# A rotation in two pieces: the scalar engine exchanges the halves, one product with a full sine table replaces two

## The chip, the cores and the metric

The kernel runs on one core of one Trainium2 chip. The metric is the device time of one execution in microseconds; times below are the median of three runs, and the time and span of one profiled execution. Engines: TensorE (PE, with its weight loads as PEld), VectorE (DVE), ScalarE (ACT), GpSimd (POOL), SyncE (SP, which here only issues transfers).

## What is computed

Four layers, each `x = x + attention(ln(x)) * silu(ffn(ln(x)))`, on 2 sequences of 512 tokens with 256 features. The change lies in the third layer's attention (and its entry), which has 16 query heads of width 128 in 4 groups; a group shares one key and one value head:

```python
q = einsum("bim,ghmd->bghid", x, w_aq); k = einsum("bim,gmd->bgid", x, w_ak); v = ...
def _rope(x):                      # angles: position * 10000 ** (-arange(64) / 64)
    even, odd = split(x, 2, axis=-1)           # two halves of 64 features
    return concatenate([even * cos - odd * sin, even * sin + odd * cos], axis=-1)
s = einsum(_rope(q) * c, _rope(k) * c) - 1e30 * (later key)      # c = 128 ** -0.25
p = softmax(s); o = einsum(p, v); r = einsum(o, w_ao)
```

## The kernel before, in words

Each engine runs a list of instructions written out by hand; semaphores order them across engines, and an instruction that waits holds back all that stands behind it on its engine.

**Steps and units.** The third attention (`attention2` on each engine) works in 32 units, one for each head and sequence, of four steps; a step u handles 128 queries against (u % 4 + 1) * 128 keys. A step passes through: scores on PE (L1126), the row maximum on DVE (`maximum`, L2259, whose result `nm` is read out by a second instruction), exp on ACT (`exponent`, L1715), the reciprocal and scaling on DVE (`inverse`, L2274 and L2276), the turn of the probabilities on PE (`turn`, L1130) and a copy on ACT (`store_pt`, the copy helper L1567). After the fourth step PE multiplies with the values (`values`, L1135), and ACT copies the result (`store_output`, L1567) at the start of the next unit. Scores run four steps ahead of turns, so a unit's four score tiles belong to the next unit.

**Projections.** q, k and v of later units are projected inside the steps, at the list positions in `EVENT2`: a q at the fourth step of a unit for three units later (until unit 28), and at the second step of four of the eight units of a group a k or a v of the next group (groups 0 to 2). All of them go through PSUM bank 7, so a projection waits (`free`) until the one before it has been read. Units are called here plain (only a q), k units (k and q: 2 in a group) and v units (v and q: 2 in a group).

**The rotation** of a projected q or k (`rotate2`, L2286 to L2290) is four instructions on DVE, placed at the end of its step: a 128x512 product with the cosines out of PSUM, two 64x512 products with the sines that read the other half of the rows out of PSUM, and the 128x512 sum in SBUF. PE waits for the third (`rope_mul`) before it uses bank 7 again.

The order of the queues in a step u is: PE `turn(u)`, `scores(u + 4)`, a projection if there is one, `values(u)` in a fourth step; ACT `exponent(u + 3)`, `store_output` in a first step, `store_v` for a v projected in the step before, `store_pt(u)`; DVE `inverse(u + 2)`, `maximum(u + 4)`, `rotate2` if there is a projection.

**The entry.** The second layer ends with eight output tiles in `shared1`: PE (L1534) makes a tile, DVE adds (`tail`, L2495), ACT takes the silu (L1897), DVE updates X (`update`, L2478 and L2479). After four tiles DVE takes the statistics of the first half (`ln_stats`, L1971 and L1974), POOL the root (`ln_rstd`, L583 and L584), DVE scales the first half (`ln_scale`, L1981). PE turns this half (`ln_transpose`, L808) ahead of the last two output tiles, and ACT copies it (`ln_copy`) between two silus. Then the second half goes the same way, while PE projects the first sequence's q, k, v (L1119, L1112) and DVE rotates. POOL splits the turned tokens into high and low parts (L734, L735; the sum of both is used from the second head on), and later every q and k weight (L739, L740).

Of the kernel before, what the change touches and what calls it, by code (L numbers as in the profile page):

```python
# [22 lines left out]
ALU = mybir.AluOpType  # L23
# [16 lines left out]
DH = 128  # L40
# [23 lines left out]
def build(nc, W, out):  # L64
    ctx = ExitStack()
    with ctx:
# [16 lines left out]
        def sem(name):  # L83
            return ctx.enter_context(nc.semaphore(name))
# [54 lines left out]
        spare2 = W2[:, 7168:10240]  # L139
        ks2 = [ks, [spare2[:, 512 * b:512 * b + 512] for b in range(B)]]  # L140
        vv2 = [vv, [spare2[:, 1024 + 512 * b:1536 + 512 * b].rearrange("p (j e) -> p j e", j=TPB) for b in range(B)]]
        rope_t = [ropet, spare2[:, 2048:2560]]
        rope_u = [ropeu, spare2[:, 2560:3072]]

# [166 lines left out]
        corea = [{k: sem(f"{k}_{l + 2}") for k in CORE_A + (() if l == 0 else ("pj_used", "w_parts"))} for l in range(2)]  # L311
        wq_in, wk_in, wv_in = sem("wq_in"), sem("wk_in"), sem("wv_in")
        xl_ready, parts_2 = sem("xl_ready"), sem("parts_2")
        rope_mul, qk_ready, v_ready = sem("rope_mul"), sem("qk_ready"), sem("v_ready")
        ot_ps, ot_sb, out_ps, s_ready = sem("ot_ps"), sem("ot_sb"), sem("out_ps"), sem("s_ready")
        comb_out, comb_in = sem("comb_out"), [sem(f"comb_in_{i}") for i in range(2)]
# [100 lines left out]
        def nth_qk(e):  # L417

            return sum(1 for x in PJ2[:e] if x[0] != "v")
# [147 lines left out]
        def _(pool):  # L567
            steps = [0]

            def own(ins):  # L570

                steps[0] += 1
                ins.then_inc(pool_step, 1)
                pool.wait_ge(pool_step, steps[0])
# [156 lines left out]
            for b in range(B):  # L731
                t = slice(b * SEQ, (b + 1) * SEQ)
                pool.wait_ge(xnt_ready, LN_PAIRS * 2 + 2 * (b + 1))
                own(pool.tensor_copy(XH2[:, :, t], XNT[:, :, t]))  # L734
                pool.tensor_tensor(XL2[:, :, t], XNT[:, :, t], plain(XH2[:, :, t]), ALU.subtract).then_inc(parts_2, 1)  # L735
            for kind, i in SPLIT2:
# [59 lines left out]
        def _(pe):  # L796
# [373 lines left out]
            def attention2():  # L1170
                ca = corea[0]

                def free(e):

                    kind = PJ2[e][0]
                    if kind == "v":
                        pe.wait_ge(v_ready, nth_v(e) + 1)
                    else:
                        pe.wait_ge(rope_mul, nth_qk(e) + 1)

                def project(e):
                    kind, b, i, bank = PJ2[e]
# [329 lines left out]
            def shared1():  # L1512
                f = ffn[1]
                nm = len(SH1)
                for b in range(B):
                    for n, (c0, r) in enumerate(SH1):
                        k = b * nm + n
                        i = k % 2
                        if k >= 2:
                            pe.wait_ge(f["h"], k - 1)  # L1520
                        for s in range(2):
                            for c in range(DC):
                                ins = mm(PS[2 * s + i][0:r, :], sgu1[:, s, c, c0:c0 + r], XNT[:, c, b * SEQ:(b + 1) * SEQ],  # L1523
                                         start=c == 0, stop=c == DC - 1)
                        ins.then_inc(f["gu_ps"], 1)
                pe.wait_ge(s_ready, NT * 2)
                pe.wait_ge(f["h"], B * nm)
                for m in range(NT):
                    if m == NT - 2:
                        ln_transpose(2, (0, 1))  # L1530
                    if m >= 2:
                        pe.wait_ge(f["f"], m - 1)
                    for n, (c0, r) in enumerate(SH1):
                        ins = mm(PS[6 + m % 2][:, 0:D], h1[0:r, n, m * P:(m + 1) * P], sd1[0:r, n, :],  # L1534
                                 start=n == 0, stop=n == nm - 1)
                    ins.then_inc(f["y_ps"], 1)

            for l in range(4):
                if l == 0:
# [23 lines left out]
        def _(act):  # L1563
# [8 lines left out]
            def ln_copy(l, pairs=range(LN_PAIRS)):  # L1572

                for k in pairs:
                    act.wait_ge(xnt_ps, LN_PAIRS * l + k + 1)
                    src = PS[turn_bank(l, k)][:, :].rearrange("p (m c t) -> p c m t", m=2, c=DC)
                    dst = (XH3 if l == 3 else XNT)[:, :, 2 * k * P:(2 * k + 2) * P].rearrange("p c (m t) -> p c m t", m=2)
                    copy(dst, src).then_inc(xnt_ready, 1)
# [143 lines left out]
            def attention2():  # L1722
                ca = corea[0]

                def exponent(u):
                    act.wait_ge(ca["nm"], u + 1)
                    if u >= 4:
                        act.wait_ge(ca["pt_ps"], u - 3)
                    exp_tile(u).then_inc(ca["e_ready"], 1)

                def store_pt(u):
                    unit = u // TPB
                    act.wait_ge(ca["pt_ps"], u + 1)
                    if u % TPB == 0 and unit >= 2:
                        act.wait_ge(ca["o_ps"], unit - 1)
                    copy_pt(u, unit % 2).then_inc(ca["pt_sb"], 1)

                def store_v(e):
                    kind, b, i, bank = PJ2[e]
                    if kind == "v":  # L1740
                        act.wait_ge(ca["pj_ps"], e + 1)
                        copy(vv2[i % 2][b].rearrange("p j e -> p (j e)"), PS[bank][:, :]).then_inc(v_ready, 1)

                def store_output(unit):
                    head, b = unit // B, unit % B
                    act.wait_ge(ca["o_ps"], unit + 1)
                    copy(OT23[:, head, b * SEQ:(b + 1) * SEQ], PS[6][:, :]).then_inc(ca["o_used"], 1)

                store_v(2)
                ln_copy(2, (2, 3))  # L1750
                for u in range(3):
                    exponent(u)
                store_v(5)
                for u in range(STEPS2):
                    if u + 3 < STEPS2:
                        exponent(u + 3)
                    if u % TPB == 0 and u > 0:
                        store_output(u // TPB - 1)
                    if u - 1 in EVENT2:
                        store_v(EVENT2[u - 1])  # L1760
                    store_pt(u)
                store_output(NH * B - 1)

# [195 lines left out]
        def _(dve):  # L1959
# [303 lines left out]
            def attention2():  # L2263
                ca = corea[0]
                dve.wait_ge(ld["ffn2"], 32)

                def maximum(u):
                    dve.wait_ge(ca["s_ps"], u + 1)
                    max_tile(u).then_inc(ca["nm"], 1)

                def inverse(u):
                    c = u % 4
                    dve.wait_ge(ca["e_ready"], u + 1)
                    own(dve.reciprocal(erec[:, c:c + 1], esum[:, c:c + 1]))  # L2274
                    p = Pr[c][:, 0:(u % TPB + 1) * P]
                    ts(p, p, erec[:, c:c + 1], None, ALU.mult).then_inc(ca["p_ready"], 1)  # L2276

                def rotate2(e):

                    kind, b, i, bank = PJ2[e]  # L2280
                    if kind == "v":
                        return
                    n, x, hf = nth_qk(e), PS[bank], DH // 2
                    t, u = rope_t[n % 2], rope_u[n % 2]
                    dve.wait_ge(ca["pj_ps"], e + 1)
                    tt(t, x[:, :], rope2[:, 0, :], ALU.mult)  # L2286
                    tt(u[0:hf, :], x[hf:, :], rope2[hf:, 1, :], ALU.mult)
                    tt(u[hf:, :], x[0:hf, :], rope2[0:hf, 1, :], ALU.mult).then_inc(rope_mul, 1)
                    dve.wait_ge(rope_mul, n + 1)
                    tt(qs[b] if kind == "q" else ks2[i % 2][b], t, u, ALU.add).then_inc(qk_ready, 1)  # L2290

                rotate2(0)
                ln_scale(2, 1)
                rotate2(1)
                rotate2(3)
                rotate2(4)
                for u in range(4):
                    maximum(u)
                inverse(0)
                inverse(1)  # L2300
                for u in range(STEPS2):
                    if u + 2 < STEPS2:
                        inverse(u + 2)
                    if u + 4 < STEPS2:
                        maximum(u + 4)
                    if u in EVENT2:
                        rotate2(EVENT2[u])

# [358 lines left out]
def shape_tables():  # L2667
# [20 lines left out]
    c = DH ** -0.25  # L2688

    t["rope2"] = np.ascontiguousarray(np.stack([np.concatenate([np.cos(ang), np.cos(ang)], 0) * c,  # L2690
                                                np.concatenate([np.sin(ang), -np.sin(ang)], 0) * c], 1)).astype(np.float32)
    t["desc"] = np.tile((E - np.arange(E)).astype(np.float32), (P, 1))
    return t

# [54 lines left out]
```

## Time and profile before

| | us |
|---|---|
| median of 3 runs (lowest to highest) | 1256.98 (1256.3 to 1258.65) |
| profiled execution, its own time | 1254.57 |
| its span (and what lies around it) | 1252.8 (1.8) |
| PE, DVE, ACT busy in the span | 1154.7 (92%), 730.0 (58%), 592.1 (47%) |
| entry and third attention: from the last tiles of the second layer to the last unit's values | about 453 to 749 |

The share of busy time is an average over four layers. What the change is worth is read from the entry and from the 32 units: where one engine waits for another there, and for how long.

### The profile page before, as it was taken

The numbers are of one execution on the slowest core, as the hardware profiler recorded it, in microseconds if no ns is written. First come the engines' busy times: TensorE is split into PE (matmuls) and PEld (weight loads), VectorE is DVE, ScalarE is ACT, GpSimd is POOL, SyncE is SP. The second block draws the span as 40 slices with busy tenths as digits, with TensorE's granted clock in tenths as the row PEclk, the third lists the DMA queues.
The fourth block names the chain that finished last, engine by engine and source line by source line (L and its number), as shares of the span: only waits on it lengthen the run. The fifth ranks groups of instructions, "written<-read, shape, count | busy, mean of one in ns | idle before, by whom it ended". The sixth has DMA issues, their size and how long they took to land.

```text
span 1252.8 us, 18479 instructions
## 1 busy us (share of the span) xinstructions
PE 1154.7 (92%) x6272; PEld 788.1 (63%) x6276; DVE 730.0 (58%) x2031; ACT 592.1 (47%) x1494; POOL 211.1 (17%) x265
## 2 busy tenths in 40 slices
PE   5979988988999978999999999999999999999999
PEld 4635454523267555666767668877777777776877
DVE  2878726846234278989898853434444444446574
ACT  1735553677832223455545543415555555555140
POOL 3150013521500413000100012010211021110000
PEclk9989999999999998999999999999999999999999
DMA  8001100050222500000000010220000000000001
GB/s 231 35 2 48 49 30 1 11 177 1 70 82 81 185 0 18 13 14 9 13 9 10 9 68 26 78 86 9 22 22 17 18 26 18 19 9 2 0 1 34
DMA packets 26896, 48.66 MB, mean 39 GB/s; under 512 B 3774, under 2 KB 20126, under 8 KB 25734
## 3 DMA queue, kind: packets, MB, share of 16 engines
q1 hardware_dynamic: 24070, 38.13, 9.5%
q0 software_dynamic: 2736, 9.37, 2.6%
q8 instruction: 52, 0.85, 0.3%
q14 instruction: 38, 0.31, 0.1%
HBM read 40.36 MB, written 9.19 MB: 40 GB/s over the span
## 4 chain that ended last, share of the span: by engine, by line
PE 73%; DVE 15%; ACT 6%; issue 4%; POOL 1%; DMA 1%; SPq 0%; ACTq 0%; DVEq 0%; POOLq 0%
PE bank L1135 9%; PE bank L1126 8%; PE bank L1319 8%; PE bank L1130 5%; PE bank L1364 4%; PE bank L1233 4%; PE bank L1314 4%; PE bank L1194 3%; PE bank L1472 2%; PE bank L1039 2%; PE bank L1028 2%; ACT PT L1686 2%; PE bank L1523 2%; PE bank L1490 2%; PE bank L949 1%
## 5 line engine op out<-in xcount | busy, mean ns | idle before, releaser
L2259 DVE CUSTOM_DVE_ANT_0 bank<-bank,mask_row 128x128 f32<-128x128 f32 (+3 forms) x256 | 126.7, 496 | 147.5 <-PE bank L1126 147.0
L1567 ACT COPY R<-bank 128x512 f32<-128x512 f32 (+5 forms) x175 | 94.9, 555 | 217.5 <-PE bank L1135 123.5
L1715 ACT ACTIVATE R<-bank,nm 128x128 f32<-128x128 f32 (+3 forms) x256 | 136.3, 532 | 112.7 <-DVE nm L2259 111.6
L1126 PE MATMUL bank<-R 128*128 128x512 f32 (+3 forms) x384 | 134.3, 434 | 0.0
L1567 ACT COPY PT<-bank 128x128 f32<-128x128 f32 (+3 forms) x256 | 108.5, 425 | 22.9 <-PE bank L1130 22.9
L1130 PE MATMUL bank<-identf,R 128*128 128x128 f32 x640 | 112.2, 274 | 6.2 <-DVE R L2276 6.1
L1130 PEld LDWEIGHTS bank<-identf,R 128*128 128x128 f32 x640 | 79.2, 141 | 37.5 <-DVE R L2276 20.0
L1135 PE MATMUL bank<-PT,R 128*128 128x512 f32 (+3 forms) x256 | 74.7, 435 | 5.9 <-ACT PT L1567 5.9
L1686 ACT ACTIVATE PT<-bank 128x512 f32<-128x512 f32 x128 | 66.5, 608 | 14.1 <-PE bank L1028 14.1
L1135 PEld LDWEIGHTS bank<-PT,R 128*128 128x128 f32 x256 | 47.5, 189 | 35.1 <-issue 15.4
L2161 DVE TENSOR_REDUCE W<-bank 128x1 f32<-128x128 f32 (+3 forms) x128 | 57.0, 485 | 17.7 <-PE bank L905 16.8
L2276 DVE TENSOR_SCALAR R<-R,erec 128x128 f32<-128x128 f32 (+3 forms) x128 | 56.1, 438 | 5.2
L1126 PEld LDWEIGHTS bank<-R 128*128 128x128 f32 x384 | 58.2, 191 | 1.4 <-issue 0.8
L1675 ACT ACTIVATE PT<-bank 128x512 f32<-128x512 f32 (+3 forms) x128 | 45.8, 437 | 25.4 <-PE bank L938 25.2
L1233 PE MATMUL bank<-W,R 128*128 128x256 f32 x256 | 55.8, 379 | 0.4 <-ACT R L1567 0.4
L1364 PE MATMUL bank<-W,R 128*128 128x256 f32 x256 | 55.8, 379 | 0.4 <-ACT R L1567 0.4
L2322 DVE TENSOR_SCALAR R<-R,erec 128x128 f32<-128x128 f32 (+3 forms) x128 | 52.7, 412 | 5.1
L1364 PEld LDWEIGHTS bank<-W,R 128*128 128x128 f32 x256 | 48.4, 190 | 7.1 <-issue 0.6
L1233 PEld LDWEIGHTS bank<-W,R 128*128 128x128 f32 x256 | 48.4, 190 | 7.1 <-issue 0.6
L1028 PE MATMUL bank<-R 96*128 96x512 bf16 x128 | 42.1, 392 | 11.0 <-ACT PT L1686 7.2
L1715 ACT ACTIVATION_READ_ACCUMULATOR R<-bank,nm 128x1 f32 x256 | 50.4, 197 | 0.0
L1028 PEld LDWEIGHTS bank<-R 96*128 96x128 bf16 x128 | 10.5, 97 | 55.7 <-ACT PT L1686 50.1
(363 smaller groups left out, 2524.0 us busy)
## 6 DMA issues: line engine op xcount, KB each, us to landing
W<-in_wq SPq DMA_DIRECT2D x32, 128.0 KB, 2.0
W<-in_wo SPq DMA_DIRECT2D x2, 2048.0 KB, 8.1
W<-in_egu SPq DMA_DIRECT2D x1, 2816.0 KB
W<-in_wk SPq DMA_DIRECT2D x20, 128.0 KB, 2.0
R<-xg SPq DMA_DIRECT2D x5, 512.0 KB, 4.6
yg<-R SPq DMA_DIRECT2D x5, 512.0 KB, 3.3
W<-in_wa SPq DMA_DIRECT2D x2, 1024.0 KB, 5.4
W<-in_wb SPq DMA_DIRECT2D x2, 1024.0 KB, 7.1
```

Of the source, the lines that this page charges most:

```text
L1028: mm(PS[n % 3][:, :], kstk[0:KQ, g, b * SEQ + j * P:b * SEQ + (j + 1) * P], qstk[0:KQ, g * GH + h, b * SEQ:(b + 1) * SEQ], start=True, sto ...
L1126: return mm(PS[u % 4][:, 0:n], q[:, t * P:n], k[:, 0:n], start=True, stop=True)
L1130: ins = tr(PS[4 + u % 2][:, j * P:(j + 1) * P], Pr[u % 4][:, j * P:(j + 1) * P], identf[:, :])
L1135: ins = mm(PS[6][:, j * P:SEQ], v[:, j, :], PT[:, slot, j, j * P:SEQ], start=j == 0, stop=j == TPB - 1)
L1233: ins = mm(PS[OUT_BANK2[m]][:, 0:D], OT23[:, k, m * P:(m + 1) * P], wo23[:, k, :], start=k == 0, stop=k == NH - 1)
L1319: ins = mm(bank[:, :], w[:, c, :], x[:, c, b * SEQ:(b + 1) * SEQ], start=c == 0 and k == 0, stop=c == DC - 1 and k == 2)
L1364: ins = mm(PS[OUT_BANK3[m]][:, 0:D], OT23[:, k, m * P:(m + 1) * P], wo23[:, k, :], start=k == 0, stop=k == NH - 1)
L1567: return nc.scalar.copy(dst, src)
L1686: fn(PT[:, s % 2, h, :], PS[n % 3][:, :], ACT.Exp, scale=HD ** -0.5).then_inc(cb["pb_ready"], 1)
L1715: return fn(Pr[c][:, 0:n], PS[c][:, 0:n], ACT.Exp, scale=-1.0, bias=nm[:, c:c + 1], accum_out=esum[:, c:c + 1])
L2161: dve.tensor_reduce(nmx[b][:, t, h:h + 1], PS[banks[i % len(banks)]][:, 0:(t + 1) * P], AX.X, ALU.max, negate=True).then_inc(smax_used, 1)
L2259: return dve.tensor_tensor_reduce(out=s[:, 0:n], in0=s[:, 0:n], in1=mask_row[:, SEQ - n:SEQ], scale=-1.0, scalar=-MASKED, op0=ALU.add, op1 ...
```

## The change

The rotation is cut in two. `rotate2` keeps only the product with the cosines. ACT copies the two halves of the projected tile, exchanged, out of bank 7 into a buffer (`swap_halves`, two 64x512 copies, after the cosine product and after the step's `store_pt`). `rotate2_rest`, two steps later on DVE, multiplies that buffer by a full 128-row sine table (one 128x512 product, all in SBUF) and adds. The next projection into the bank now also waits for the two copies (`swap_ready`). At the entry the first transposes stand behind the last two output tiles, POOL's first split waits until all tokens are scaled, and the first four rotations are reordered with the copies among ACT's.

```diff
@@ POOL: split of the tokens
                 pool.wait_ge(xnt_ready, LN_PAIRS * 2 + 2 * (b + 1))
+                pool.wait_ge(xn_ready, NT * 3)
                 own(pool.tensor_copy(XH2[:, :, t], XNT[:, :, t]))
@@ PE: free(e), before a bank is used again
                         pe.wait_ge(rope_mul, nth_qk(e) + 1)
+                        pe.wait_ge(swap_ready, 2 * nth_qk(e) + 2)
@@ PE: shared1
                 for m in range(NT):
-                    if m == NT - 2:
-                        ln_transpose(2, (0, 1))
...
                     ins.then_inc(f["y_ps"], 1)
+                ln_transpose(2, (0, 1))
@@ ACT: attention2
+                def swap_halves(e):
+                    kind, b, i, bank = PJ2[e]
+                    if kind != "v":
+                        n, hf = nth_qk(e), DH // 2
+                        act.wait_ge(rope_mul, n + 1)
+                        if n >= 2:
+                            act.wait_ge(qk_ready, n - 1)
+                        copy(swapped[n % 2][0:hf, :], PS[bank][hf:, :]).then_inc(swap_ready, 1)
+                        copy(swapped[n % 2][hf:, :], PS[bank][0:hf, :]).then_inc(swap_ready, 1)
+
+                swap_halves(0)
+                swap_halves(1)
                 store_v(2)
                 ln_copy(2, (2, 3))
+                swap_halves(3)
+                swap_halves(4)
...
                     if u - 1 in EVENT2:
                         store_v(EVENT2[u - 1])
+                        if PJ2[EVENT2[u - 1]][0] != "v":
+                            store_pt(u)
+                            swap_halves(EVENT2[u - 1])
+                            continue
                     store_pt(u)
@@ DVE: attention2
-                    t, u = rope_t[n % 2], rope_u[n % 2]
-                    dve.wait_ge(ca["pj_ps"], e + 1)
-                    tt(t, x[:, :], rope2[:, 0, :], ALU.mult)
-                    tt(u[0:hf, :], x[hf:, :], rope2[hf:, 1, :], ALU.mult)
-                    tt(u[hf:, :], x[0:hf, :], rope2[0:hf, 1, :], ALU.mult).then_inc(rope_mul, 1)
+                    t = rope_t[n % 2]
+                    if n >= 2:
+                        dve.wait_ge(qk_ready, n - 1)
+                    dve.wait_ge(ca["pj_ps"], e + 1)
+                    tt(t, x[:, :], rope2[:, 0, :], ALU.mult).then_inc(rope_mul, 1)
+
+                def rotate2_rest(e):
...
+                    t, u = rope_t[n % 2], rope_u[n % 2]
+                    dve.wait_ge(swap_ready, 2 * n + 2)
+                    own(tt(u, swapped[n % 2], rope2[:, 1, :], ALU.mult))
                     dve.wait_ge(rope_mul, n + 1)
                     tt(qs[b] if kind == "q" else ks2[i % 2][b], t, u, ALU.add).then_inc(qk_ready, 1)

                 rotate2(0)
                 ln_scale(2, 1)
                 rotate2(1)
+                rotate2_rest(0)
+                rotate2_rest(1)
                 rotate2(3)
                 rotate2(4)
+                rotate2_rest(3)
+                rotate2_rest(4)
...
                         maximum(u + 4)
+                    if u - 2 in EVENT2:
+                        rotate2_rest(EVENT2[u - 2])
                     if u in EVENT2:
                         rotate2(EVENT2[u])
```

The sine table's two halves change sign to match, and the exchange buffer `swapped` (two of 128x512) takes free room in W2. The `own` helper makes DVE wait for its own instruction's end.

## Rows read from the trace of the kernel before

**Rows 1.** Stretch of units: start:end, length, busy PE, PEld, DVE, ACT, POOL; PEclk, DMA.

```profile
500.00:570.00 70.00, 66.39 (x315) 45.87 (x314) 61.39 (x178) 35.94 (x108) 6.55 (x10) 1.00 0.04 12
```

**Rows 2.** Timeline of PE: where `values` starts (start, us, idle before in brackets).

```profile
494.98 2.42 PE L1135 MATMUL bank<-PT,R 128*128 128x512 f32 x8 [1.18 <-ACT PT L1567]
...
537.33 2.32 PE L1135 MATMUL bank<-PT,R 128*128 128x512 f32 x8
545.92 2.32 PE L1135 MATMUL bank<-PT,R 128*128 128x512 f32 x8
...
561.39 2.32 PE L1135 MATMUL bank<-PT,W 128*128 128x512 f32 x8
571.11 2.42 PE L1135 MATMUL bank<-PT,W 128*128 128x512 f32 x8 [1.19 <-ACT PT L1567]
...
693.71 2.32 PE L1135 MATMUL bank<-PT,W 128*128 128x512 f32 x8
...
731.10 2.42 PE L1135 MATMUL bank<-PT,W 128*128 128x512 f32 x8 [0.67 <-ACT PT L1567]
```

**Rows 3.** Timeline of all engines in one plain unit.

```profile
703.82 0.69 DVE L2290 TENSOR_TENSOR R<-R 128x512 f32<-128x512 f32 x1
703.85 0.59 ACT L1567 COPY R<-bank 128x512 f32<-128x512 f32 x1 [1.97 <-PE bank L1135]
...
704.33 0.27 ACT L1567 COPY PT<-bank 128x128 f32<-128x128 f32 x1
...
705.09 0.55 PE L1130 MATMUL bank<-identf,R 128*128 128x128 f32 x3 [0.30 <-DVE R L2276]
...
706.11 0.16 DVE L2274 RECIPROCAL erec<-esum 128x1 f32<-128x1 f32 x1
...
706.51 0.56 DVE L2259 CUSTOM_DVE_ANT_0 bank<-bank,mask_row 128x384 f32<-128x384 f32 x1
...
707.16 0.58 ACT L1715 ACTIVATE R<-bank,nm 128x384 f32<-128x384 f32 x1
...
707.74 0.58 ACT L1567 COPY PT<-bank 128x512 f32<-128x512 f32 x1
```

**Rows 4.** Groups by form, 484 to 737 us (count, busy us, mean ns, idle before).

```profile
L1567 ACT COPY R<-bank 128x512 f32<-128x512 f32 x33 | 19.3, 585 | 57.2 <-PE bank L1135 57.2
...
L740 POOL TENSOR_TENSOR wq_low<-W,wq_high 128x256 fp32r<-128x256 f32 x14 | 13.3, 953 | 1.1
...
L2287 DVE TENSOR_TENSOR W<-bank,W 64x512 f32<-64x512 f32 x18 | 12.5, 692 | 0.2
```

**Rows 5.** Timelines of DVE, ACT and PE at the entry.

```profile
457.07 1.38 DVE L1981 TENSOR_SCALAR XN<-X,mv,rstd 128x256 f32<-128x256 f32 x4 [0.55 <-POOL rstd L584]
461.86 0.48 DVE L2495 SCALAR_TENSOR_TENSOR R<-bank,sgate,PT 128x256 f32<-128x256 f32 x1 [3.41 <-PE bank L1534]
...
466.70 0.38 DVE L1974 BATCH_NORM_AGGREGATE mv<-stat 128x2 f32<-128x6 f32 x4
...
469.99 3.39 DVE L1981 TENSOR_SCALAR XN<-X,mv,rstd 128x256 f32<-128x256 f32 x4
...
460.35 0.42 ACT L1897 ACTIVATE R<-R 128x256 f32<-128x256 f32 x1
...
475.43 6.74 PE L1119 MATMUL bank<-XNT,W 128*128 128x512 f32 x8 [0.68 <-ACT XNT L1567]
```

**Rows 6.** Timeline of POOL at the entry.

```profile
467.48 1.04 POOL L584 TENSOR_TENSOR rstd<-rstd,mhalf 128x4 f32<-128x4 f32 x1
...
469.60 2.66 POOL L735 TENSOR_TENSOR x_low<-XNT,x_high 128x1024 fp32r<-128x1024 f32 x1
```

**Rows 7.** TensorE's clock: a PE timeline row, two windows (PEclk third from the end).

```profile
64.86 3.40 PE L840 MATMUL bank<-identb,PT 128*96 128x128 bf16 x32 [2.55 <-DVE PT L2089]
...
66.00:68.00 2.00, 2.00 (x22) 2.00 (x20) 0.56 (x1) 1.66 (x2) 2.00 (x1) 0.50 0.00 0
...
476.00:478.00 2.00, 2.00 (x3) 0.67 (x2) 0.11 (x1) 0.00 (x0) 1.92 (x2) 0.50 0.03 8
```

More of the change, by code:

```diff
@@ L141, in build @@
         vv2 = [vv, [spare2[:, 1024 + 512 * b:1536 + 512 * b].rearrange("p (j e) -> p j e", j=TPB) for b in range(B)]]
+        swapped = [W2[:, 6144 + 512 * i:6656 + 512 * i] for i in range(2)]
         rope_t = [ropet, spare2[:, 2048:2560]]
@@ L313, in build @@
         xl_ready, parts_2 = sem("xl_ready"), sem("parts_2")
+        swap_ready = sem("swap_ready")
         rope_mul, qk_ready, v_ready = sem("rope_mul"), sem("qk_ready"), sem("v_ready")
@@ L2282, in rotate2 @@
                         return
-                    n, x, hf = nth_qk(e), PS[bank], DH // 2
+                    n, x = nth_qk(e), PS[bank]
+                    t = rope_t[n % 2]
[4 more added lines that the diff above has]
+                def rotate2_rest(e):
+                    kind, b, i, bank = PJ2[e]
+                    if kind == "v":
+                        return
+                    n = nth_qk(e)
                     t, u = rope_t[n % 2], rope_u[n % 2]
-                    dve.wait_ge(ca["pj_ps"], e + 1)
-                    tt(t, x[:, :], rope2[:, 0, :], ALU.mult)
-                    tt(u[0:hf, :], x[hf:, :], rope2[hf:, 1, :], ALU.mult)
-                    tt(u[hf:, :], x[0:hf, :], rope2[0:hf, 1, :], ALU.mult).then_inc(rope_mul, 1)
+                    dve.wait_ge(swap_ready, 2 * n + 2)
+                    own(tt(u, swapped[n % 2], rope2[:, 1, :], ALU.mult))
                     dve.wait_ge(rope_mul, n + 1)
@@ L2690, in shape_tables @@
     t["rope2"] = np.ascontiguousarray(np.stack([np.concatenate([np.cos(ang), np.cos(ang)], 0) * c,
-                                                np.concatenate([np.sin(ang), -np.sin(ang)], 0) * c], 1)).astype(np.float32)
+                                                np.concatenate([-np.sin(ang), np.sin(ang)], 0) * c], 1)).astype(np.float32)
     t["desc"] = np.tile((E - np.arange(E)).astype(np.float32), (P, 1))
```

## The prediction

> **What bounds the kernel now.** I read the busy time by stretches first. In the units PE is busy 66.4 of 70 us, DVE 61.4, ACT 35.9 [rows 1]: PE is the bound, DVE is close behind it, ACT has room, and there are only some 3.6 us of idle PE in 70 to be won. Then the timeline of PE at the value products, which end a unit: from 494.98 to 693.71 lie 24 units (three groups of eight, 66.24 each), from there to 731.10 five more (37.39) [rows 2]. A k unit takes 9.72, of which PE idles 1.19 waiting for the copy of the turned probabilities [rows 2] (the row at 571.11); a v unit takes 8.59 with no idle time (537.33 to 545.92) [rows 2]. With two of each in a group, 29.6 are left for the four plain units, 7.4 each. The third view is all engines in one plain unit [rows 3], where I follow the order of the queues; the fourth, the entry on DVE, ACT and PE [rows 5], where DVE idles 3.41 for output tiles that stand behind the transposes.
>
> **The entry.** With the transposes moved back, the last two tiles are ready before DVE asks for them, so the 3.41 of idle time go [rows 5]. Next comes the silu of the sixth tile, which ACT takes only after copying the transposes, at 460.35 [rows 5]. Before, the addition at 461.86 was followed after 4.84 by the aggregate of the statistics (466.70). If the chain now starts from the silu's end (460.77) without the addition's own 0.40, the aggregate comes at 465.2, 1.5 earlier; without the gap PE should turn and ACT copy 0.75 sooner. I take 2.2 between (bounds 1.5 and 2.3). POOL's root ended at 468.52, but the scaling began only at 469.99 because four rotation instructions stood ahead [rows 5, 6]; one is left, 1.4 gained. The scaling took 3.39 beside POOL's split (469.60, 2.66 long), 1.38 where POOL rested [rows 5, 6]: with the split held back, 2.0. Holding it back delays the split little (it starts with the scaling's end, about 467.8 against 468.5), and its user, the second head's projection, is over 10 us away. Against this, from the scaling's end to the second sequence's projections at 475.43 passed 2.05; now one product (0.65), two copies (1.10), the copy of v (0.48) and the two transposed copies (1.07) follow in turn, 3.3, so 1.25 is given back. After the projections (6.75) DVE needed 2.8 for the last rotation; now one product and two rests follow, about 3.5: another 0.7 back. Sum 2.2 + 1.4 + 2.0 - 1.25 - 0.7 = 3.7 gained (bounds 2.9 and, with the clock below, 6.7).
>
> In the first unit the rotation no longer stands before the maxima; the idle 1.18 at 494.98 [rows 2] goes, as the copies end before PE wants the bank: 1.3 with the shorter first product, bounds 0 and 1.5.
>
> **The rotation in the units.** Removed: two 64x512 products of 0.69 (L2287) [rows 4]; added on DVE: one product from SBUF, 0.69 by the nearest row, the sum of the same form (L2290) [rows 3]. DVE's gain of 0.7 per rotation is worth only what PE's idle time is. Added on ACT: two copies of 64x512. No row has one; a 128x512 copy takes 0.585 [rows 4], and the next starts 0.48 after it (703.85 to 704.33) [rows 3]. From below, half the rows might cost half (0.29); but 64-row products cost DVE the same 0.69 as the 128-row sum [rows 3, 4]. I take the full price: 0.48 + 0.585 = 1.07 for the pair. The Trainium skill (ScalarE: Activation LUTs, What ACT_TABLE_LOAD costs) prices an instruction by the elements in a row alone, 186 ns and 0.833 ns for each, less 93 ns between neighbours: 1.13 for the pair as an estimate, which would add 1.7 to the sum below.
>
> Where the copies stand decides. A q is projected just before the values; its copies stand on ACT behind the output copy and the first probabilities' copy of the next unit. Both wait for PE: the output copy starts at 703.85, when the values have ended. So the pair can't start before about 704.53 (704.33 and 0.20 for the small copy) and ends at 705.60.
>
> What waits for it first is PE. In a k or v unit the k or v projection is next in the bank. PE is through with its first turns and scores by 704.79 (the turn at 705.09 less its idle 0.30 [rows 3]), somewhat sooner in a stream, so it stands for 0.9 to 1.0. Before, the third product had ended by the values' end. A v unit becomes 8.59 + 1.0 = 9.6. A k unit loses its old wait and gets this: 9.72 - 1.19 + 0.95 = 9.5.
>
> What waits second is DVE. In a plain unit the rest stands behind the second maximum and ahead of the third; behind it are an inverse and that maximum, behind the maximum the third exp, behind this on ACT the copy of the fourth probabilities, and for that copy the values wait. That closes a ring from one output copy to the next:
>
> 0.48 output copy + 0.20 small copy + 1.07 exchange + 0.04 + 1.34 rest (two of 0.69, neighbours overlapping) + 0.40 inverse (706.11 to 706.51) + 0.65 maximum to exp (706.51 to 707.16) + 0.58 exp (to 707.74) + 0.58 copy + 0.05 + 2.42 values after a wait + 0.04 = 7.85 [rows 2, 3].
>
> The unit shown takes about 7.4, and PE's own work in it is under 7. After a unit whose values didn't wait it is 0.1 less; mean in a group 7.75. Before, the same ring had no exchange in it: the rotation ran under the values, and nothing after them waited for ACT.
>
> So a group is 2 x 9.5 + 2 x 9.6 + 4 x 7.75 = 69.2, 3.0 more than 66.24; three groups 8.9. The five units after them, each with an exchange left over, take 39.3 against 37.4, 1.9. The last unit has none. Together 10.8 lost, less 3.7 and 1.3: 5.8. Profiled time 1254.57 + 5.8 = 1260.4. The median of the runs shown is 2.4 above the profiled time, so the forecast is 1256.98 + 5.8 = **1262.8**. A link that is 0.1 longer or shorter moves 17 plain units, 1.7; with the entry's bounds this gives 1259.5 to 1267 for this case.
>
> The new sine product reads both operands from SBUF, the two old ones read one from PSUM. For the first two rests POOL's split runs beside them; even at the scaling's ratio (3.39 to 1.38) they are done before the last projections end, which hides it.
>
> **Rivals.**
> - *Half the rows cost half* (faster). If the exchange takes 0.53 instead of 1.07, PE's stand shrinks by 0.54 in 12 units (6.5), and the rest starts 0.28 earlier in 17 (then the second maximum binds it, 4.8): 5.8 - 11.3 = -5.5, 1251.5. It decides from a pair of about 0.87 on, 0.2 less than I take. Against it, the 64-row products. Chance 0.17.
> - *TensorE stays at 2.4 GHz in the entry.* At 476 to 478 the granted clock was 0.50, that is 1.2 GHz, after PE stood idle [rows 7]; now it stands idle for about 2.0, works 1.2 and idles 2.7 ahead of those projections. If the clock holds, they take some 3 less: +2.8, 1259.8. But it also fell, to 0.50 at 66 to 68, around a gap of 2.55 (the row at 64.86) [rows 7]. Chance 0.15. In the units the gaps stay near 1, and with 1.19 the clock was 1.00 [rows 1, 2].
> - *POOL blocks the rest.* 14 splits of 0.95 [rows 4]; if each met a rest and took 0.75 per us, as the split did from the scaling, +10: 1273. Against it, they should run in the unit's first microseconds, before the rest. The Trainium skill (SBUF — State Buffer, Who interferes with whom) has a DVE instruction with two SBUF operands blocked while GpSimd reads SBUF; 3.39 against 1.38 shows such a loss, for another form. Chance 0.08.
>
> **How the numbers follow.** The ring has 0.55; 0.05 is for what I don't see. The range, 1253 to 1269, leaves out most of the first rival and the third, about 2 in 10. A measurement here tells 0.2%, 2.5 us, from no change. Faster 0.18 (the first rival), same 0.19 (half of the second, the ring's lower end), slower 0.63.
>
> **What would show it.** Right: the exchange's copies at 0.58 each, right behind the first small copy; PE waiting for ACT's copies 12 times for about 1.0 before k and v projections; value products waiting about 0.9 for ACT in plain units, spaced 7.75 to 7.85; DVE's idle time ahead of the rest; the scaling at 1.4. Wrong: copies of 0.3, value products 7.0 to 7.4 apart, or the second projections in the entry at full clock.

## The result, and the profile after

The changed kernel takes 1268.85 us (median of 8 runs, 1265.36 to 1274.68), the kernel before 1256.64 beside it (8 runs, 1255.51 to 1259.06): a ratio of 1.0102, 95% interval [1.0083, 1.0121]. That is 12.2 us slower between the medians, where 5.8 were forecast. The direction was right; the forecast size was a little under half of the measured one. The median lies inside the stated range, 1253 to 1269, just under its upper end.

The profiled execution took 1271.36 (its span is 1269.5), 16.8 more than the one before. I cut both traces at the same places: the first aggregate of the statistics at the entry, the first value product, the value products that end the 24 units and the next five, and the end of the span.

| us | before | after | difference | forecast |
|---|---|---|---|---|
| start to the first aggregate | 454.99 | 454.65 | -0.3 | 0 |
| from there to the first values (entry, first unit) | 39.99 | 37.01 | -3.0 | -5.0 |
| 24 units | 198.73 | 214.69 | +16.0 | +8.9 |
| five more units | 37.39 | 40.19 | +2.8 | +1.9 |
| the rest of the kernel | 521.65 | 523.00 | +1.3 | 0 |

The differences add up to the 16.8. This execution lies 2.5 above the median of its own runs, and the one before lay 2.1 below, so 16.8 and 12.2 don't contradict each other. The start, up to the first aggregate, where no edit lies, takes from 450.25 to 455.00 in the eleven traces of this document. So comparisons below go by stretches inside a trace.

The timeline of PE after, at value products and at one v projection:

```profile
491.66 2.32 PE L1138 MATMUL bank<-PT,R 128*128 128x512 f32 x8
...
608.60 2.32 PE L1138 MATMUL bank<-PT,W 128*128 128x512 f32 x8
613.01 2.02 PE L1115 MATMUL bank<-W,XNT 128*128 128x128 f32 x16 [1.11 <-issue]
618.53 2.32 PE L1138 MATMUL bank<-PT,W 128*128 128x512 f32 x8
...
706.35 2.42 PE L1138 MATMUL bank<-PT,W 128*128 128x512 f32 x8
714.38 2.42 PE L1138 MATMUL bank<-PT,W 128*128 128x512 f32 x8
...
746.54 2.42 PE L1138 MATMUL bank<-PT,W 128*128 128x512 f32 x8 [1.24 <-ACT PT L1570]
```

These answer to [rows 2]. A v unit (608.60 to 618.53) takes 9.93 where it took 8.59, and PE, which had no idle time in it, waits 1.11 in front of the v projection. A plain unit (706.35 to 714.38) takes 8.03.

Busy time in the same stretch of units as [rows 1], and in four microseconds of the first unit (PEclk third from the end):

```profile
500.00:570.00 70.00, 62.23 (x294) 42.53 (x295) 49.52 (x152) 44.87 (x124) 5.74 (x10) 1.00 0.04 12
484.00:488.00 4.00, 4.00 (x14) 3.13 (x14) 1.62 (x7) 1.77 (x8) 0.00 (x0) 0.57 0.02 4
```

PE's busy time falls from 66.4 to 62.2 of 70 and DVE's from 61.4 to 49.5, while ACT's grows from 35.9 to 44.9. The work went from DVE to ACT as meant, all three engines now have room, and the units are longer: they wait for one another. The second row shows a fall of TensorE's granted clock (0.57) in the first unit, where the trace of before has 1.00; it lies in the entry's row of the table. Another (0.59 from 860 to 864), which the trace of before doesn't have either, lies in the last row.

All engines in one plain unit after, which answers to [rows 3]:

```profile
716.84 0.58 ACT L1570 COPY R<-bank 128x512 f32<-128x512 f32 x1 [1.80 <-PE bank L1138]
717.33 0.27 ACT L1570 COPY PT<-bank 128x128 f32<-128x128 f32 x1
717.62 1.19 ACT L1570 COPY W<-bank 64x512 f32<-64x512 f32 x2
718.83 0.37 ACT L1718 ACTIVATE R<-bank,nm 128x128 f32<-128x128 f32 x1
718.84 0.69 DVE L2318 TENSOR_TENSOR R<-W 128x512 f32<-128x512 f32 x1 [0.36 <-ACT W L1570]
719.19 0.36 ACT L1570 COPY PT<-bank 128x256 f32<-128x256 f32 x1
719.70 0.63 PE L1133 MATMUL bank<-identf,R 128*128 128x128 f32 x4 [0.79 <-ACT PT L1570]
720.57 0.56 DVE L2280 CUSTOM_DVE_ANT_0 bank<-bank,mask_row 128x384 f32<-128x384 f32 x1
721.22 0.58 ACT L1718 ACTIVATE R<-bank,nm 128x384 f32<-128x384 f32 x1 [0.83 <-DVE nm L2280]
721.79 0.58 ACT L1570 COPY PT<-bank 128x512 f32<-128x512 f32 x1
722.42 0.30 PEld L1138 LDWEIGHTS bank<-PT,W 128*128 128x128 f32 x2 [0.29 <-ACT PT L1570]
722.42 2.42 PE L1138 MATMUL bank<-PT,W 128*128 128x512 f32 x8
```

The ring of the prediction can be followed here: output copy 716.84, small copy 717.33, exchange 717.62, rest 718.84, third maximum 720.57, exp 721.22, copy 721.79, values 722.42, and the next output copy at 724.88, 8.04 later. Two links are longer than forecast: the exchange starts 0.29 behind the small copy and not 0.20, and the rest 1.22 behind the exchange's start and not 1.11. The others agree within 0.05.

But the values wait only 0.29 here (the row of their weight loads), where 0.9 was forecast. PE spends the rest of the waiting earlier, 0.79 ahead of the fourth step's turns (719.70), for a copy of probabilities that stands behind the exchange on ACT. The waits that ended last, for 500 to 753 (us, times, longest):

```profile
PE bank L1133 <- ACT PT L1570: 13.4, 17, 0.8
...
PE bank L1115 <- issue: 6.7, 6, 1.1
...
PE bank L1198 <- issue: 5.6, 5, 1.1
```

The lower two are PE's stand for the bank, ahead of v (L1115) and k projections (L1198); the profile names nothing there, but with one copy less a v unit is 0.61 shorter (experiment 7). The first, 17 times 0.8, was not in the forecast. The chain that ended last, for 716 to 723, goes through it and not through DVE at all:

```profile
717.33 0.27 ACT PT L1570
...
718.23 0.58 ACT W L1570
...
719.29 0.27 ACT PT L1570
...
719.70 0.63 PE bank L1133 x4
720.33 0.86 PE bank L1129 x2
721.18 1.37 PE bank L1198 x6
722.56 0.56 PE bank L1138
```

So there is a second ring: output copy, small copy, exchange, the first exp and the second tile's copy of the next step on ACT, then PE's turns, scores, projection and values, and the output copy again. Both rings pass through the exchange. Which of them holds the unit is what the experiments had to tell.

### The profile page after: what moved, and what is told of

It reads as the page before. It is cut to its first block, busy times and chain, and to the rows that moved or that the text cites. A ratio compares the mean times of both kernels' runs of the same rounds, so it can differ in the third digit from the quotient of the medians.

```text
span 1269.5 us, 18637 instructions
## 1 busy us (share of the span) xinstructions
PE 1159.2 (91%) x6272; PEld 786.4 (62%) x6276; DVE 705.2 (56%) x1991; ACT 635.3 (50%) x1574; POOL 207.7 (16%) x265
## 4 chain that ended last, share of the span: by engine, by line
PE 76%; DVE 8%; ACT 7%; issue 6%; POOL 1%; DMA 1%; SPq 0%; ACTq 0%; DVEq 0%; POOLq 0%
PE bank L1138 11%; PE bank L1129 8%; PE bank L1323 8%; PE bank L1368 4%; PE bank L1237 4%; PE bank L1133 4%; PE bank L1198 4%; PE bank L1318 4%; PE bank L1476 2%; PE bank L1042 2%; PE bank L1031 2%; ACT PT L1689 2%; PE bank L1527 2%; PE bank L1494 2%; PE bank L952 1%
## 5 line engine op out<-in xcount | busy, mean ns | idle before, releaser
L1133 PEld LDWEIGHTS bank<-identf,R 128*128 128x128 f32 x640 | 78.9, 141 | 49.5 <-issue 35.1
L1689 ACT ACTIVATE PT<-bank 128x512 f32<-128x512 f32 x128 | 66.4, 610 | 14.1 <-PE bank L1031 14.1
L1570 ACT COPY W<-bank 64x512 f32<-64x512 f32 (+2 forms) x92 | 53.3, 580 | 38.5 <-PE bank L914 22.9
L2182 DVE TENSOR_REDUCE W<-bank 128x1 f32<-128x128 f32 (+3 forms) x128 | 57.0, 486 | 17.8 <-PE bank L908 17.0
L2297 DVE TENSOR_SCALAR R<-R,erec 128x128 f32<-128x128 f32 (+3 forms) x128 | 53.1, 415 | 5.0
L2358 DVE TENSOR_SCALAR R<-R,erec 128x128 f32<-128x128 f32 (+3 forms) x128 | 52.7, 412 | 5.1
```

Source lines behind the costliest of these rows:

```text
L1133: ins = tr(PS[4 + u % 2][:, j * P:(j + 1) * P], Pr[u % 4][:, j * P:(j + 1) * P], identf[:, :])
L1570: return nc.scalar.copy(dst, src)
L1689: fn(PT[:, s % 2, h, :], PS[n % 3][:, :], ACT.Exp, scale=HD ** -0.5).then_inc(cb["pb_ready"], 1)
L2182: dve.tensor_reduce(nmx[b][:, t, h:h + 1], PS[banks[i % len(banks)]][:, 0:(t + 1) * P], AX.X, ALU.max, negate=True).then_inc(smax_used, 1)
```

## The experiments

The theories, as numbered in the expectations: **A**, one ring, through the rest on DVE (the prediction's); **B**, a second ring of nearly the same length through ACT and PE alone; **C**, it is PE's wait for the bank that matters, and the plain units follow from it. Lengths are means of the distances between value products in the profiled execution (6 k, 12 plain, 6 v units, then five); "entry" is from the first aggregate to the first values. The medians are from several sets of runs: the kernel before took 1256.66 beside experiments 1 to 4, 1254.35 beside 5, 6, 7 and 9, and 1255.2 (one run) beside 8.

| kernel | entry | k | plain | v | last five | time, median |
|---|---|---|---|---|---|---|
| before | 39.99 | 9.90 | 7.32 | 8.58 | 7.48 | 1256.64 |
| changed | 37.01 | 9.73 | 8.03 | 9.99 | 8.04 | 1268.85 |
| entry edits only | 34.90 | 9.98 | 7.32 | 8.58 | 7.47 | 1249.2 |
| rotation only | 39.64 | 9.74 | 8.03 | 9.98 | 8.04 | 1274.44 |
| copies first | 37.23 | 8.79 | 7.58 | 8.63 | 7.53 | 1247.74 |
| rest late | 36.93 | 9.64 | 7.91 | 9.93 | 7.75 | 1266.08 |
| both moves | 36.85 | 8.32 | 7.50 | 8.59 | 7.04 | 1242.45 |
| both, old entry rotations | 33.48 | 8.33 | 7.49 | 8.59 | 7.05 | 1239.25 |
| one copy | 35.11 | 9.02 | 7.56 | 9.38 | 7.61 | 1249.19 (one run) |
| same rows | 37.03 | 9.57 | 7.91 | 9.85 | 7.91 | 1268.08 (one run) |
| split late | 40.24 | 9.73 | 8.00 | 9.99 | 8.04 | 1270.11 (one run) |

**1. The entry edits alone**, in the kernel before: the transposes behind the last output tiles, and POOL's wait.

```diff
@@ POOL
+                pool.wait_ge(xn_ready, NT * 3)
@@ shared1
-                    if m == NT - 2:
-                        ln_transpose(2, (0, 1))
...
+                ln_transpose(2, (0, 1))
```

> The kernel before with two of the entry edits alone: the first transposes behind the last output tiles, POOL's split after the scaling; the rotation stays as before, four instructions on DVE. If these two edits make the entry shorter by themselves: the first unit's values some 4 us earlier than before, units as before, about 1252.5 us. If the gain at the entry needs the shorter first rotation too (the scaling then still stands behind four products): 1 us earlier at most, 1255 to 1257.

Measured 1249.2 (1246.04 to 1253.0), ratio 0.9951 [0.9932, 0.9971]; the entry is 5.1 shorter (some 4 were expected), the units are as before. The two entry edits are a gain by themselves, and with the exchange the entry is 2.1 longer than with them alone. The trace doesn't show where the other 2.4 of the 7.5 between the medians lie.

**2. The rotation alone**, without those two edits.

```diff
@@ POOL
-                pool.wait_ge(xn_ready, NT * 3)
@@ shared1
+                    if m == NT - 2:
+                        ln_transpose(2, (0, 1))
...
-                ln_transpose(2, (0, 1))
```

> The changed kernel without those two edits. If the loss lies in the units and the two edits gain 2 to 4 us: units 18 to 19 us longer than before, slower than the changed kernel by 2 to 4, 1271 to 1274 us. If part of the loss came from the entry's order: 1266 or less.

Measured 1274.44 (1270.14 to 1275.67), ratio 1.0138 [1.0111, 1.0165]; the units as in the changed kernel, to 0.01. It is 5.6 slower than the changed kernel, where 2 to 4 were expected. The loss is the rotation's, and the parts add: 17.8 lost here less 7.5 won in experiment 1 (by the medians of those runs) is 10.3, beside 12.2.

**3. The copies first**: ACT makes the exchange ahead of the output copy and the small copy, under the values.

```diff
@@ ACT: attention2
+                    if u - 1 in EVENT2:
+                        swap_halves(EVENT2[u - 1])
                     if u % TPB == 0 and u > 0:
                         store_output(u // TPB - 1)
                     if u - 1 in EVENT2:
                         store_v(EVENT2[u - 1])
-                        if PJ2[EVENT2[u - 1]][0] != "v":
-                            store_pt(u)
-                            swap_halves(EVENT2[u - 1])
-                            continue
                     store_pt(u)
```

> The changed kernel with ACT's two copies ahead of the output copy and of the turned probabilities' copy, right after the exp, so that they run under the values. Theory A (one ring: exchange, rest on DVE, maximum, exp, copy, values): plain units 7.5, v units 8.6, k units 8.5 to 8.8, about 1245 us. Theory B (a second ring of the same length on ACT alone: exchange, exp of the first tile, copy of the second, turn of the fourth): the same here, as both lose the exchange. Theory C (only the bank wait costs): plain units stay at 8.0, v units 8.6, 1256.

Measured 1247.74 (1245.84 to 1249.75), ratio 0.9927 [0.9903, 0.9951]. The timeline of ACT and PE there:

```profile
694.40 2.42 PE L1138 MATMUL bank<-PT,W 128*128 128x512 f32 x8 [0.32 <-ACT PT L1570]
695.08 1.18 ACT L1570 COPY W<-bank 64x512 f32<-64x512 f32 x2
696.86 0.58 ACT L1570 COPY R<-bank 128x512 f32<-128x512 f32 x1 [0.59 <-PE bank L1138]
...
701.93 2.42 PE L1138 MATMUL bank<-PT,W 128*128 128x512 f32 x8 [0.32 <-ACT PT L1570]
```

The same two copies cost the same 1.18, but they lie under the values, and ACT still rests 0.59 before the output copy. A v unit falls to 8.63 and most plain ones to 7.53, not to 7.0 or so: the ring through the rest still stands, without the exchange (experiment 5 opens it). C falls, since the plain units were to keep their length by it.

**4. The rest one step later** on DVE, behind the third maximum, with the copies where the change has them.

```diff
@@ DVE: attention2
-                    if u - 2 in EVENT2:
-                        rotate2_rest(EVENT2[u - 2])
+                    if u == 3:
+                        rotate2_rest(EVENT2[1])
+                    elif u >= 6 and u - 3 in EVENT2:
+                        rotate2_rest(EVENT2[u - 3])
```

> The changed kernel with the rest of the rotation one step later on DVE (behind the third maximum instead of ahead of it; only the first rotation inside the steps keeps its place). Theory A: plain units fall from 8.0 to 7.1, v units stay at 10.0, about 1254 us. Theory B: the second ring still holds, plain units stay at 7.9 to 8.0, 1267 to 1269. Theory C: 1269.

Measured 1266.08 (1265.84 to 1266.97), ratio 1.008 [1.0058, 1.0103]. All engines in a plain unit there:

```profile
713.08 1.19 ACT L1570 COPY W<-bank 64x512 f32<-64x512 f32 x2
...
715.15 0.63 PE L1133 MATMUL bank<-identf,R 128*128 128x128 f32 x4 [0.79 <-ACT PT L1570]
715.18 0.56 DVE L2280 CUSTOM_DVE_ANT_0 bank<-bank,mask_row 128x384 f32<-128x384 f32 x1
...
715.65 0.69 DVE L2318 TENSOR_TENSOR R<-W 128x512 f32<-128x512 f32 x1
...
717.85 2.32 PE L1138 MATMUL bank<-PT,W 128*128 128x512 f32 x8
```

The third maximum now starts ahead of the rest, and the values wait for nothing; the unit is 7.91 all the same. The 0.79 that PE waits at the turns is unchanged: ring B by itself, 7.91 long, just 0.12 shorter than the changed kernel's plain units (8.03). A as the only ring falls.

**5. Both moves** together, 3 and 4.

> The change with both moves at once: the two copies ahead of the output copy, and the rest one step later on VectorE. Theory B (two rings, one through the rest on VectorE and one through the exchange on ScalarE alone): with the exchange under the values and the rest out of the way neither ring is left, and the plain units fall below those of either move alone (7.53 and 7.91), to what TensorE itself needs, 7.0 to 7.2; k units at most 8.8, v units 8.6, last five 7.1 to 7.2; about 0.4 x 17 = 7 us under the kernel with the copies first (1247.7), so 1241. Rival D: the rest, now between the third and the fourth maximum, makes the fourth maximum and the cosine product late, so that the copies run into the output copy: plain units stay at 7.5, and the time at 1247 or 1248.

Measured 1242.45 (1239.31 to 1243.66), ratio 0.99 [0.9876, 0.9923]. Busy time in the stretch of 70 us there:

```profile
500.00:570.00 70.00, 68.13 (x328) 47.51 (x327) 53.77 (x176) 50.56 (x138) 5.77 (x10) 1.00 0.04 12
```

PE is busy 68.1 of 70, more than before the change (66.4) [rows 1]: with both rings open, PE is the bound again. The plain units come at 7.17 (7.15 to 7.27), except those right behind a k unit (7.81); k units fall to 8.32. In such a plain unit the trace has two rests: the k's, which now comes a step later and so falls into this unit, and the q's. PE waits 0.46 ahead of the fourth step's turns, for the scaling that stands behind the k's rest on DVE. So the 7.50 of the table is a mean of two lengths and not D's 7.5: units with one rest lie below it, as the last five (7.04) do. D as what sets the length falls, and B stands.

**6. Both moves, and the first four rotations as before.** `rotate2_whole` is the four instructions of before (with a subtraction for the sum, as the sine table has the other sign); all later rotations are in two pieces.

```diff
@@ DVE
-                rotate2(0)
+                rotate2_whole(0)
                 ln_scale(2, 1)
-                rotate2(1)
-                rotate2_rest(0)
...
+                rotate2_whole(1)
+                rotate2_whole(3)
+                rotate2_whole(4)
@@ ACT
-                swap_halves(0)
...
-                swap_halves(4)
```

> The kernel with both moves, and the first four rotations (at the entry) with the four instructions of before, all others in two pieces. From the aggregate of the first statistics to the first values passed 39.99 us before, 37.01 with the change and 34.90 with the two entry edits alone, so the exchange and the rests cost 2.1 at the entry: if that is right, 34.9 again and 2 us less than the kernel with both moves, about 1239. Rival: the 2.1 is a fall of the clock in one execution only, then the two kernels agree within 1 us.

Measured 1239.25 (1237.28 to 1240.6), ratio 0.9878 [0.9856, 0.9899], the fastest kernel here. The entry is 3.4 shorter than with both moves, the medians differ by 3.2 (2 were expected). Of the 3.4, 1.75 lie ahead of the first maximum, which comes 24.84 behind the first aggregate and not 26.59, and 1.6 between it and the first values: with both moves the granted clock was 0.58 from 484 to 488, here it is 1.00 from 480 to 488.

**7. One copy**, to see whether a unit pays for the length of the exchange.

```diff
                         copy(swapped[n % 2][0:hf, :], PS[bank][hf:, :]).then_inc(swap_ready, 1)
-                        copy(swapped[n % 2][hf:, :], PS[bank][0:hf, :]).then_inc(swap_ready, 1)
+                        if n < 4:
+                            copy(swapped[n % 2][hf:, :], PS[bank][0:hf, :]).then_inc(swap_ready, 1)
```

> The change, but from the fifth rotation on only one of the two copies is made (the lower half of the exchanged tile is left out, so those rows hold old data). If the length of the exchange is what the units pay, plain units fall by one copy's 0.60 from 8.03 to 7.43, v units from 9.99 to 9.4, k units from 9.73 to 9.1 or 9.2. If the wait and the hand-over between engines count and not the copies' length, they stay within 0.2 of 8.03 and 9.99.

The second copy is left out, so half of the buffer holds old data. V units take 9.38, k units 9.02, plain units 7.42 where the changed kernel has 7.93 and 7.53 where it has 8.04. One copy less is 0.61 less in a v unit, 0.71 in a k unit and 0.51 in a plain one: what the units pay is the length of the exchange, in the plain ones not quite all of it.

**8. The same rows**, to see why the two copies don't overlap.

```diff
-                        copy(swapped[n % 2][0:hf, :], PS[bank][hf:, :]).then_inc(swap_ready, 1)
-                        copy(swapped[n % 2][hf:, :], PS[bank][0:hf, :]).then_inc(swap_ready, 1)
+                        copy(swapped[n % 2][0:hf, :], PS[bank][0:hf, :]).then_inc(swap_ready, 1)
+                        copy(swapped[n % 2][hf:, :], PS[bank][hf:, :]).then_inc(swap_ready, 1)
```

> The change, but the two copies move each half to the same rows and not to the other half's (so the halves are not exchanged). If two copies of 64 rows stand 0.60 apart because they cross rows, the pair comes down to 1.07 (starts 0.48 apart, as between the 128-row copies) and plain units to about 7.9. If it is so for any two copies of half the rows, or for any two that read the same bank, the pair stays at 1.18 and plain units at 8.03.

The timeline of ACT there:

```profile
698.48 0.27 ACT L1570 COPY PT<-bank 128x128 f32<-128x128 f32 x1
698.64 1.19 ACT L1570 COPY W<-bank 64x512 f32<-64x512 f32 x2
699.86 0.37 ACT L1718 ACTIVATE R<-bank,nm 128x128 f32<-128x128 f32 x1
```

The halves are not exchanged here. Neither answer is whole. The pair stays at 1.19, and what follows starts 1.22 after its start, as in the changed kernel. But the pair comes 0.16 behind the small copy and not 0.29, and the plain units fall by about as much, from 8.03 to 7.91. So the rows cost the first copy its overlap with the instruction ahead; whether by crossing to the other half, or by being read from row 64 on, this run doesn't separate. Why the second still doesn't overlap stays open: it begins in other rows than the first, and it reads the same bank.

**9. POOL's split late**, behind the first four rotations.

```diff
-                pool.wait_ge(xn_ready, NT * 3)
+                pool.wait_ge(qk_ready, 4)
                 own(pool.tensor_copy(XH2[:, :, t], XNT[:, :, t]))
```

> The change, but GpSimd's split of the tokens waits until the first four rotations are done. If that split is what slows the rests at the entry (1.20, 2.72, 1.52, 2.72 where the units have 0.69 to 0.85), all four pieces come at 0.69 to 0.8, and from the aggregate of the first statistics to the first maximum pass about 24.9 us and not 26.6. What follows is later, as the second head's projection needs the split. If the rests are slow for a reason of their own, they stay at 1.2 and 2.7.

First the timelines of DVE, POOL and PE at the entry of the changed kernel, which answer to [rows 5, 6]:

```profile
454.65 0.38 DVE L1995 BATCH_NORM_AGGREGATE mv<-stat 128x2 f32<-128x6 f32 x4
464.14 0.38 DVE L1995 BATCH_NORM_AGGREGATE mv<-stat 128x2 f32<-128x6 f32 x4
466.06 1.38 DVE L2002 TENSOR_SCALAR XN<-X,mv,rstd 128x256 f32<-128x256 f32 x4 [0.97 <-POOL rstd L586]
467.96 1.20 DVE L2318 TENSOR_TENSOR R<-W 128x512 f32<-128x512 f32 x1
468.70 2.66 POOL L738 TENSOR_TENSOR x_low<-XNT,x_high 128x1024 fp32r<-128x1024 f32 x1
469.20 2.72 DVE L2320 TENSOR_TENSOR R<-R 128x512 f32<-128x512 f32 x1
471.83 1.52 DVE L2318 TENSOR_TENSOR W<-W 128x512 f32<-128x512 f32 x1
473.39 2.72 DVE L2320 TENSOR_TENSOR R<-W 128x512 f32<-128x512 f32 x1
481.23 0.29 DVE L2280 CUSTOM_DVE_ANT_0 bank<-bank,mask_row 128x128 f32<-128x128 f32 x1
483.52 0.33 PE L1133 MATMUL bank<-identf,R 128*128 128x128 f32 x1 [3.15 <-DVE R L2297]
```

Then the same with the split late:

```profile
450.25 0.38 DVE L1995 BATCH_NORM_AGGREGATE mv<-stat 128x2 f32<-128x6 f32 x4
...
463.57 0.68 DVE L2318 TENSOR_TENSOR R<-W 128x512 f32<-128x512 f32 x1
464.29 0.69 DVE L2320 TENSOR_TENSOR R<-R 128x512 f32<-128x512 f32 x1
464.91 0.69 DVE L2318 TENSOR_TENSOR W<-W 128x512 f32<-128x512 f32 x1
465.63 0.69 DVE L2320 TENSOR_TENSOR R<-W 128x512 f32<-128x512 f32 x1
475.19 0.29 DVE L2280 CUSTOM_DVE_ANT_0 bank<-bank,mask_row 128x128 f32<-128x128 f32 x1
```

With POOL at rest all four pieces take 0.69, and the first maximum comes 24.94 after the first aggregate and not 26.58. The split was what slowed them, and it made the first maximum 1.6 later. As expected, what follows is late now, and the entry as a whole is 3.2 longer: the second head's projection waits 2.10 for POOL's parts of the weights, which stand behind the split, and the first scalings of the probabilities on DVE, now beside the split, take 0.94 to 2.38 where the changed kernel has 0.29 to 0.49.

## Why the prediction was right in sign and short in size

**The step that failed** is "the rotation in the units", and in it sizes, not the mechanism: 18.8 lost in the 29 units where 10.8 were forecast. Plain units: 0.28 each over the forecast mean of 7.75 (3.4 in twelve), and 0.9 together in the last five. 0.2 of the 0.28 are two links, the small copy (0.20 taken, 0.29 measured) and the exchange to the rest (1.07 and 0.04 taken, 1.22 measured): I took the exchange's copies to overlap with their neighbours as the 128-row copies do [rows 3], and they don't. For the first copy experiment 8 ties this to its rows, for the second the cause is open. The remaining 0.1 is the discount, which holds only for the two plain units of a group that follow a k unit (7.93); the others take 8.04, and in the first two groups one takes 8.26 and 8.47, where the trace has rests of 1.02, and of 0.82 and 1.10, beside POOL's splits. V units: 0.39 each (2.3 in six). The v projection starts 1.71 behind the scores ahead of it, 0.43 in the kernel before: PE stands for 1.28 and not for the 0.9 to 1.0 of the forecast. Of the 0.33 over its middle, 0.2 are the later end of the exchange (1.97 behind the output copy's start, 1.75 forecast) and 0.1 the step from the copy's end to the projection's start, which the sum left out. The projection itself then takes 2.02 and not 1.95. K units: 0.23 each (1.4), by the same stand; the forecast also started from a short one (9.72, where the mean of the six is 9.90).

**What I didn't see** is the second ring. It didn't set the size (at 7.91 it is the shorter of the two), but it decides what mends the kernel: by the prediction, moving the rest would have been enough, and it gains 0.12 a unit. The sign that the prediction named, "value products waiting about 0.9 for ACT", failed in just this way: the wait was there, but 0.79 of it stood at the fourth turns.

**The entry** gave 3.0 and not 5.0, and two misses that were not counted on cancel in part, which is luck. The aggregate came 2.2 sooner (9.49 after the first one, 11.71 before), the scaling began 1.4 sooner behind it and took 1.38 and not 3.39, all as forecast to 0.1; 1.4 were given back ahead of the second projections (1.25 forecast). These projections took 5.31 and not 6.74, a gain of 1.4 that the sum didn't have: the granted clock was back at full earlier (0.73 over their last four microseconds, 472 to 476, where the kernel before has 0.55, 478 to 482). Against it, from their end to the first maximum 5.0 passed and not 2.8, so 2.2 were given back where 0.7 were forecast. Here the sentence failed that the last projections hide the slow rests: these took 1.20, 2.72, 1.52 and 2.72, and the two products behind them came late; 1.6 of the loss is theirs (experiment 9). The Trainium skill (SBUF — State Buffer, Who interferes with whom) says that a DVE instruction with two SBUF inputs contends with a GpSimd instruction that reads SBUF; the trace agrees, 2.72 against 0.69 for the same instruction. The old rotation has one such instruction, the sum, the new one two. And the first unit lost 0.4 where 1.3 were to be gained: PE stood idle for 3.15 ahead of its first turn (483.52), and the granted clock fell to 0.57 from 484 to 488. From the first maximum to the first values pass 10.0 in the kernel before and 10.4 in the changed one. With the rotation only (experiment 2), where the clock stays at 1.00 there, it is 8.9: 1.1 less than before, so the step that was forecast at 1.3 holds but for the clock.

**The rest of the kernel**: +1.3. The last row of the first table is 523.0 to 523.4 in the six traces that have the fall of the clock after the units (0.59 from 860 to 864 in the changed kernel), and 521.6 to 521.7 in the five that don't, the one before among them. What brings it on I didn't try.

**Rivals.** Half the rows at half the price: wrong, the 64-row copies take 0.58 each (66 of them, mean 580 ns). TensorE at full clock in the entry: in part, it was granted 0.50 from 468 to 472 and was at full from 476 on; the projections gained 1.4 where the rival had some 3. Later it fell again, as said. In the one-copy kernel that second fall is missing (PE idles 2.64 ahead of the first turn there), and the entry is 1.9 shorter. POOL blocking the rests: in the units hardly (means of 692 to 719 ns, three above 0.8), at the entry yes, where I had called it hidden.

## What to carry to other kernels

An instruction moved to an engine with room is free only if it lies off every loop that closes through that engine: here the kernel is 12 us slower than before with the two copies behind the output copy, and 9 us faster with them ahead of it. Of these 9, the entry edits alone give 7.5 (experiment 1): the 29 units are only 3.0 shorter than before with the copies first, and 9.4 with both moves. Look for all loops through the place, not the first that fits; two of nearly equal length hide each other, and mending one of them gains almost nothing (0.12 a plain unit here, against 0.86 for both where nothing else binds). And where a small edit comes with a big one, time them apart: the two entry edits were a gain of 0.5% that the exchange buried.

## What the runs showed of the hardware

- Two 64x512 copies out of one PSUM bank to SBUF start 0.61 apart, and the next instruction starts 0.60 after the second; behind a 128x512 copy the next starts 0.48 later [rows 3]. A pair of 128x512 copies takes 1.08 (469.77, entry of the changed kernel), the pair of 64x512 ones 1.18 to 1.19. So half the rows cost no less. The Trainium skill (ScalarE: Activation LUTs, What ACT_TABLE_LOAD costs) lets neighbours overlap by about 93 ns, 1.13 for the pair as an estimate; the measurement is 0.05 more.
- Ahead of the first copy the overlap comes back when it stays in its own rows (0.16 and not 0.29 after the small copy).
- A DVE sum of two SBUF tiles took 2.72 beside GpSimd's split and 0.69 without it, and the split 2.66 beside the rests and 2.34 with DVE idle (477.08, before). A scaling of one tile was slowed by the split too: 2.38 for 128x384 with the split late, 0.42 in the changed kernel.
